# Two buffers for the scaled rows of h, a new order of the row statistics, and 65 columns for the low exponentials

## The reference

```python
def fp4_quant_dequant(x):                # blocks of 16 numbers of the last dimension
    scale = max(jnp.max(jnp.abs(xb), axis=-1, keepdims=True) / 6.0, 1e-12)
    idx = jnp.searchsorted(_MID, jnp.abs(xb / scale))
    return (_GRID[idx] * jnp.sign(xb) * scale).reshape(shape)

def ffn(x, w_gate, w_up, w_down):        # 256 -> 704 -> 256, fp4_linear quantises both sides
    h = silu(fp4_linear(x, w_gate)) * fp4_linear(x, w_up)
    return fp4_linear(h, w_down)

def attn(x):                             # 16 heads of 64
    w = softmax(q @ k.T / 64 + causal)
    w = w * mask                         # mask: one number per key and head, between 0 and 1
    w = w / (w.sum(-1, keepdims=True) + 1e-8)
    return (w @ v) @ Wo

x = x + 0.5 * ffn(layernorm(x)); x = x + attn(layernorm(x)); x = x + 0.5 * ffn(layernorm(x))
```

## Time and profile before

| | |
|---|---|
| median of 3 runs | 4051.02 us (4048.67 to 4053.14) |
| the profiled execution | 4053.32 us, of which the span from first to last instruction is 4051.3 |
| mean granted clock of TensorE in it, as a share of 2.4 GHz | 0.97 |
| busy share of the span: PE, PEld, DVE, ACT, POOL | 90%, 81%, 76%, 59%, 20% |
| first feed-forward pass | from about 100 to 600 us |
| attention | from about 600 to 3510 us |
| second feed-forward pass | from about 3510 us to the end |

### The profile page before, as it was taken

One profiled execution on the slowest core, in us unless ns is written; L12 is line 12 of the kernel. 1 busy time (PEld: TensorE's weight loads), 2 busy tenths in 40 slices (PEclk: granted clock), 3 DMA queues, 4 the chain that ended last, 5 costly groups with the idle time before them and its releaser, 6 DMA issues. The chain is left out here.

```text
span 4051.3 us, 90034 instructions
## 1 busy us (share of the span) xinstructions
PE 3636.0 (90%) x29924; PEld 3264.7 (81%) x29924; DVE 3089.6 (76%) x4884; ACT 2380.1 (59%) x5622; POOL 824.1 (20%) x830
## 2 busy tenths in 40 slices
PE   0899996998999899889989988998998899599998
PEld 0899995887788788778878877887787788489998
DVE  7999984777677677767766776776677677599997
ACT  1444443776676577667766766676676667344444
POOL 2222321211121111112111111121121112122222
PEclk9999998999999999999999999999999999799999
DMA  6111104443443444344444434343443434211111
GB/s 208 42 55 47 57 32 128 109 97 84 124 118 84 116 104 103 84 116 110 101 101 108 112 84 116 94 117 90 110 109 88 113 91 115 86 35 55 47 52 34
DMA packets 160295, 372.54 MB, mean 92 GB/s; under 512 B 19552, under 2 KB 59360, under 8 KB 159456
## 3 DMA queue, kind: packets, MB, share of 16 engines
q1 hardware_dynamic: 159968, 368.73, 35.2%
HBM read 128.79 MB, written 38.54 MB: 41 GB/s over the span
## 5 line engine op out<-in xcount | busy, mean ns | idle before, releaser
L1213 ACT ACTIVATE at_eT_hi<-at_t_ps 128x512 f16<-128x512 f32 (+3 forms) x1536 | 753.9, 493 | 582.9 <-PE at_t_ps L1125 542.4
L1294 DVE SCALAR_TENSOR_TENSOR at_eT_lo<-at_t_ps,at_eT_hi 128x512 f16<-128x512 f32 (+3 forms) x1536 | 830.7, 553 | 241.7 <-ACT at_eT_hi L1213 158.5
L1205 ACT ACTIVATE at_e_rows<-at_s_ps,at_neg_max 128x1024 f32<-128x1024 f32 (+7 forms) x1024 | 767.6, 750 | 109.1 <-DVE at_neg_max L1288 108.7
L1288 DVE TENSOR_REDUCE at_neg_max<-at_s_ps 128x1 f32<-128x1024 f32 (+7 forms) x1024 | 767.8, 750 | 49.2 <-PE at_s_ps L1115 39.9
L1125 PE MATMUL at_t_ps<-at_ident,at_e_rows 128*128 128x128 f32 x4608 | 779.7, 279 | 21.7 <-DVE at_eT_lo L1294 18.3
L1139 PE MATMUL at_o_ps<-at_v_cols,at_eT_hi 128*128 128x130 f16 x4608 | 694.2, 221 | 16.7 <-ACT at_o_raw L1221 15.0
L1139 PE MATMUL at_o_ps<-at_v_cols,at_eT_lo 128*128 128x130 f16 x4608 | 693.9, 220 | 0.0
L1111 PE MATMUL at_s_ps<-at_kh_st,at_q_st 128*128 128x512 f32 (+2 forms) x1536 | 587.7, 383 | 49.8 <-issue 25.1
L1125 PEld LDWEIGHTS at_t_ps<-at_ident,at_e_rows 128*128 128x128 f32 x4608 | 511.4, 143 | 58.1 <-DVE at_eT_lo L1294 33.7
L1112 PE MATMUL at_s_ps<-at_kl_st,at_q_st 128*128 128x512 f32 (+2 forms) x1536 | 520.1, 346 | 0.0
L1139 PEld LDWEIGHTS at_o_ps<-at_v_cols,at_eT_hi 128*128 128x128 f16 x4608 | 449.6, 98 | 31.8 <-ACT at_o_raw L1221 18.0
(11 more groups left out here) (184 smaller groups left out, 7491.0 us busy)
## 6 DMA issues: line engine op xcount, KB each, us to landing
at_kh_st<-at_k_hi SPq DMA_DIRECT2D x256, 256.0 KB, 4.4
at_kl_st<-at_k_lo SPq DMA_DIRECT2D x256, 256.0 KB, 5.8
at_w_qk<-w_qk_split SPq DMA_DIRECT2D x64, 512.0 KB, 6.1
at_q_st<-at_q_hi SPq DMA_DIRECT2D x128, 256.0 KB, 3.9
at_q_st<-at_q_lo SPq DMA_DIRECT2D x128, 256.0 KB, 4.9
at_w_v<-w_v_split SPq DMA_DIRECT2D x66, 256.0 KB, 5.7
at_w_out<-w_out_split SPq DMA_DIRECT2D x64, 256.0 KB, 5.7
ffn_x_rows<-in_L_attn_query_dram SPq DMA_DIRECT2D x32, 256.0 KB, 2.8
```

Source lines behind the costliest of these rows:

```text
L1205: nc.scalar.activation(e_rows[:, n % 4, :w], s_ps[n % 2][:, col:col + w], ACT.Exp, bias=neg_max[:, n % 4:n % 4 + 1], accum_out=e_sum[:, pa ...
L1213: nc.scalar.activation(eT[0][:, i % EBUF, :count * P], t_ps[i % 2][:, :count * P], ACT.Copy, scale=PSCALE).then_inc(sem("eT_hi"), 1)
L1288: nc.vector.tensor_reduce(neg_max[:, n % 4:n % 4 + 1], s_ps[n % 2][:, col:col + P * (j + 1)], AX.X, ALU.max, negate=True).then_inc(sem("ma ...
L1294: nc.vector.scalar_tensor_tensor(out=eT[1][:, i % EBUF, :count * P], in0=t_ps[i % 2][:, :count * P], scalar=PSCALE, in1=eT[0][:, i % EBUF, ...
```

## The change

Five things are changed, and what is computed stays the same but for one term.

1. `h_q` gets two buffers, chosen by the macro's parity. Product j of macro m on GpSimd waits for `h_turned` of macro m-2 instead of m-1.
2. On VectorE `to_units` is cut in two: `block_max(i)` with the maximum, and `to_units(i)` with the rest. `row_stats(i+4)` stands between them instead of at the head of `body`.
3. On GpSimd `root(i+4)` stands behind `scale_inner` and `scale_rows` instead of ahead of them.
4. `row_norm` of the macros 1 to 3 waits for the `unit` step before it.
5. In the attention the low exponentials are multiplied with the first 65 of `v_cols` (the high parts of v and mask) instead of all 130. The term low exponential x low part is no longer computed.

```diff
-        h_q = sb("h_q", [P, 2, IPAD])
+        h_q = sb("h_q", [P, 2, 2, IPAD])
...
             def row_norm(m, k):
+                if isinstance(m, int) and 1 <= m <= AHEAD_X:
+                    dve.wait_ge(sem("unit"), m)
                 dve.wait_ge(sem("rstd"), m + 1)
...
-            def to_units(i, par):
+            def block_max(i):
...
                 nc.vector.tensor_reduce(amax[:, blk], blocks_of(raw[:, a:b]), AX.X, ALU.max, apply_absolute_value=True).then_inc(sem("amax"), 1)
+
+            def to_units(i, par):
+
+                a, b = set_cols(i)
+                blk = slice(a // QB, b // QB)
                 dve.wait_ge(sem("amax"), i + AHEAD_X + 1)
...
             def body(i, k, r):
-                if has(i + 4):
-                    row_stats(i + 4, k, r + 1)
                 if has(i):
                     inner(i, 0)
...
                 if has_set(i):
+                    block_max(i)
+                if has(i + 4):
+                    row_stats(i + 4, k, r + 1)
+                if has_set(i):
                     to_units(i, k % 2)
...
-                if has(m - 1):
-                    pool.wait_ge(sem("h_turned"), 2 * m + j - 1)
-                nc.gpsimd.tensor_tensor(blocks_of(h_q[:, j, :INNER]), blocks_of(code[:, j * INNER:(j + 1) * INNER]),
+                if has(m - 2):
+                    pool.wait_ge(sem("h_turned"), 2 * m + j - 3)
+                nc.gpsimd.tensor_tensor(blocks_of(h_q[:, par, j, :INNER]), blocks_of(code[:, j * INNER:(j + 1) * INNER]),
...
             def body(i, k, r):
-                if has(i + 4):
-                    root(i + 4, k % 2)
                 if has(i - 1):
                     for j in range(2):
                         scale_inner(i - 1, j, (k + 1) % 2)
                 if has(i + 2):
                     scale_rows(i + 2, (k + 1) % 2)
+                if has(i + 4):
+                    root(i + 4, k % 2)
...
-                    last = turn(hT_ps[:, kt * P:(kt + 1) * P], h_q[:, j, kt * P:(kt + 1) * P], kt % 4 == 0, False)
+                    last = turn(hT_ps[:, kt * P:(kt + 1) * P], h_q[:, par, j, kt * P:(kt + 1) * P], kt % 4 == 0, False)
...
+VPART = (VCOLS, DH + 1)
...
-                        last = nc.tensor.matmul(o_ps[:, :VCOLS], eT[s][:, i % EBUF, b * P:(b + 1) * P], v_cols[par][:, k0 + b, a, :],
+                        last = nc.tensor.matmul(o_ps[:, :VPART[s]], eT[s][:, i % EBUF, b * P:(b + 1) * P], v_cols[par][:, k0 + b, a, :VPART[s]],
                                                 start=k0 + b == 0 and s == 0, stop=k0 + b == j and s == 1)
```

More of the change, by code:

```diff
@@ L297, in _ @@
         def _(dve):
-            nc.vector.memset(h_q[:, :, INNER:], 0.0).then_inc(sem("pad_zeroed"), 1)
+            nc.vector.memset(h_q[:, :, :, INNER:], 0.0).then_inc(sem("pad_zeroed"), 1)
             nc.vector.memset(power[:], -0.5).then_inc(sem("power"), 1)
@@ L500, in rest_rows, with turn_inner @@
                                  skip_group_check=True).then_inc(sem("x_rest"), 1)
-            def turn_inner(m, j):
+            def turn_inner(m, j, par):
                 pe.wait_ge(sem("h_q"), 2 * m + j + 1)
@@ L551, in body @@
                 if has(i - 2):
-                    turn_inner(i - 2, 0)
+                    turn_inner(i - 2, 0, k % 2)
                 if has(i):
@@ L563, in body @@
                 if has(i - 2):
-                    turn_inner(i - 2, 1)
+                    turn_inner(i - 2, 1, k % 2)
                 if has(i + 1):
```

## The result

The changed kernel takes **3947.35 us** (median of 4 runs, 3943.77 to 3950.1) beside 4051.99 us for the kernel before: a ratio of 0.9743, 95% interval 0.9726 to 0.9759. Measured once more beside later runs, it took 3944.06 us (3942.76 to 3947.6) beside 4051.42: 0.9737 (0.9724 to 0.975). The forecast was 3942 in 3896 to 4008. The profiled execution took 3950.1 us, 103.2 less than the one before.

A forecast was written before the change was run, and what follows sets the result against it. VectorE was taken to bound the feed-forward macros, with TensorE a close second, and TensorE the attention. From the profiled 4053.3 us, 38, 10 and 62 came off, giving 3943, against the median 3941; forecast 3942, range 3896 to 4008.

The forecast's parts named there:

- The bound and the steady macros: Feed-forward: VectorE's cycle falls from 15.48 to 14.5 us, below TensorE's 14.79; 55 stalls of 0.69 us vanish, 38 us gained.
- wait for coarse: Feed-forward, VectorE: `total` would be ready before ScalarE's coarse step ends and wait about 0.4 us per macro.
- (a): Feed-forward, VectorE: row statistics move from behind `unit` to behind the block maximum; the stretch of 1.67 us shrinks to 0.27.
- (b): Feed-forward, GpSimd: a second `h_q` buffer lets the second product start without waiting 1.18 us for the transposes.
- (c): Feed-forward, GpSimd: the root goes behind the products; costed at nothing, with a whole macro until row_norm needs it.
- The root: its rival: Feed-forward: the root blocks `tied` and `scale`, adding 0.78 us to VectorE every macro; 27 us less gain, about 3969; chance 0.12.
- The attention: TensorE's low products shrink from 130 to 65 columns, saving 0.027 us each except last ones: 83 us, of which 62 arrive.
- The three quarters: Attention: estimated share of the 83 us saved on low products that reaches the end, 62 us; growing waits eat the rest.
- Of its rival: Attention: the low product gets no shorter because load or issue needs 0.055 us anyway; about 4003 us, chance 0.17.
- last products save nothing: Attention: each group's last low product precedes a 32-bit load of 0.10 us, so 12 of 36 per head gain nothing.
- The starts: Start of each feed-forward pass: first-block steps go before the DMA wait, so TensorE starts earlier; 5 and 5, 10 us.
- The rival by the clock: Attention: shorter TensorE streams lower the clock from 2.4 to 1.2 GHz for part of each pair; slower, chance 0.07.

The follow-up runs named there:

- copy_first: Changed kernel, with ScalarE copying the first block's transposed rows before the next block's coarse step at each feed-forward pass's start: 3940.1 us, ratio 0.9724.

## Why the prediction was right, and where it was not

- **The bound and the steady macros: right.** VectorE's own cycle fell below TensorE's. 38 us were forecast, 55 stalls of 0.69; the marks show 36.1 and 34.5. The product was a little large, for seven of the 55 stalls stand at the starts of the passes, and there they stayed; the 48 others of the same trace are 33.4 us. The macro came out at 14.72 against a forecast of 14.8. `total` got its wait for coarse (0.31; 0.4 forecast), and it cost nothing, as forecast.
- **Which edit does it: left open by the prediction, settled by the runs in part.** It argued with (a), and gave (b) no price of its own. (b) alone, or (a) and (c) together, makes TensorE the bound, and beside (a) and (c) the buffer (b) is worth nothing.
- **The root: its rival was hardly put to the test, though the root matters.** The rival wanted a tensor_scalar of VectorE to wait for the root. In a steady macro `tied` and `scale` have both started when the root does (340.27 and 340.41, against 340.44), so they could not have waited for it. What speaks against the rival are the norms of the earlier trace rows, themselves tensor_scalars, the second of which starts inside a root; the reciprocal, a step of another kind, starts inside the root too and takes its usual 0.89. That no macro paid is thus in part luck of the order of starts. The prediction costed the root's new place at nothing. That is right for the kernel as changed, but had it been left where it was, the statistics' new place would have turned the gain into a loss of 18 us.
- **The attention: right in cause, and in size with some luck.** 62 us forecast; 62.3 and 66.3 by the marks, 61 alone. The low product gave up 0.027 us, as forecast. The three quarters said to arrive were an estimate that no row supports, and that they came so close is luck. The assumption that a 16-bit load fits in 0.027 us held, narrowly: the floor is about 0.027 to 0.03. For it the prediction had only one pair of products. Of its rival it said that the trace never shows instructions closer than 0.055, and that is not so: behind the same low product the score product starts after 0.03 (3384.17). Here the Trainium skill, "TensorE: Matmul & The Clock Gate", section "Back-to-back issue gap", which has about 81 ns for a load with its product of 128 columns in a stream, would have forbidden the gain, and the trace did not agree with it: 0.056 us with 130 columns, 0.029 with 65. That last products save nothing held too. The weight loads' waits for the low exponentials grew by 13.2 us (33.7 to 46.9), of the some 21 of the 83 us that did not arrive; how the rest divides was not measured.
- **The starts: the term that was mis-sized.** The sum took 10 us; they gave 4.7 in one profiled execution and 7.6 in the other, and the feed-forward part has 7 over the second buffer alone (4011.01 and 4018.43), most of it there. The prediction followed the chain from the DMA over VectorE and GpSimd to TensorE's first transposes and stopped there, at 105.00. The next link is ScalarE, whose copy stands behind a coarse step. Moving the statistics ahead of `tied` put the DMA's wait into exactly the `unit` which that coarse step needs. `copy_first` gave 4 to 7 us of it back.
- **The rest.** The terms forecast 110 us between profiled executions, 103.2 were measured; the starts account for 5.3 of the 7 and the steady macros for 1.9. With the second profiled execution it is 108.4: starts and steady macros stay 2.4 and 3.5 below their terms, and the attention is 4.3 above its own. That the sum is met to a few us is certain, then, but not which term carries the difference. The rival by the clock did not show: it is 1.00 from 1109 to 1148 us after the change as in the earlier trace rows, and its mean over the two executions is 0.96 and 0.97, with 0.97 before.

## What to carry to other kernels

When a step that can wait for a DMA moves, follow everything that then queues behind it on its own engine, and from each of these on to the other engines' queues, until a product of the bounding engine has started; stopping at its first instruction is too early. When an engine's stall is taken away in two ways at once, price each alone against the next bound: a gain ends there, and the second edit may be worth nothing. An edit that gains nothing by itself may still be what keeps another from doing harm, as the root's new place did here. When two executions of one kernel are both profiled, divide the time with each: a part of a few us, as the starts here (4.7 and 7.6), can differ by half of itself. In this kernel a short product pays only next to a short load: put it where the following load is short, and hide a long one behind a long load.

## What the runs showed of the hardware

- VectorE and GpSimd stand still for one another, a whole instruction at a time, and only for some kinds of work. Beside GpSimd's product of 128x512 a tensor_scalar of VectorE waits for its end, even on 2 numbers (`var_eps`, 0.58 instead of 0.17 us). With the root ahead of the products, `unit` waited for one product of 704 columns (3.07 us instead of 2.16), and the next one waited for `unit` (3.30 instead of 1.39). Beside h (0.88) and the residual (0.69), which read PSUM, and the block maximum (2.14), the same products took 1.39 each, as in the kernel before, and VectorE's steps kept their lengths. All this agrees with the Trainium skill, "SBUF — State Buffer", section "SBUF: two separate sides": it has the shared port pair locked for a whole instruction, between an instruction of GpSimd and one of VectorE that uses both ports or has two inputs in SBUF. Whether a tensor_scalar is one that uses both ports, no trace shows.
- The root, a power of 2 columns, does not agree with it, though it reads SBUF as well. The norms of the earlier trace rows kept their length beside it, and so did a `unit` on 512 columns at the start of a pass after the change, begun 0.42 us into a root; without a root beside it, it takes 0.69 us too (92.22 in the kernel before).

```profile
92.78 0.69 POOL L409 TENSOR_TENSOR ffn_rstd<-ffn_var_eps,ffn_power 128x2 f32<-128x2 f32 x1 [2.83 <-DVE ffn_var_eps L312]
```

```profile
93.20 0.69 DVE L352 TENSOR_TENSOR ffn_unit<-ffn_raw,ffn_recip 128x512 f32<-128x512 f32 x1
```

- A 16-bit weight load with a short product behind it takes about 0.03 us in the stream, with 65 columns (0.029) nearly as with 33 (0.027); a 32-bit load takes 0.10 to 0.11 us and hides a product of 65 or 130 columns.
